# Dividing the attention output by its row sums between two DVE block transposes, with a projection in two halves, in a fused attention and mixture-of-experts kernel

## What is computed

```python
q, k, v = (proj(Wq), proj(Wk), proj(Wv))          # each (b, 16, 512, 8)
q = _l2norm(q); k = _l2norm(k)
sim = einsum('bhid,bhjd->bhij', q, k) * SCALE     # causal mask, SCALE = 8
attn = _softmax(sim)
o = einsum('bhij,bhjd->bhid', attn, v).transpose(0, 2, 1, 3).reshape(b, n, d)
return einsum('bnf,fd->bnd', o, Wo)
```

## Time and profile before

| what | us |
|---|---|
| three runs | 796.7, 798.49, 802.25 (median 798.49) |
| the profiled execution | 802.14 |
| its span, first to last instruction | 800.4 |
| PE busy | 716.7 (90%) |
| DVE busy | 491.1 (61%) |
| ACT busy | 495.4 (62%) |
| POOL busy | 431.9 (54%) |

### The profile page before, as it was taken

How to read it: one execution, slowest core, us unless ns; L and a number is a source line. 1 busy time by engine, 2 the same in 40 slices (tenths; PEclk the granted TensorE clock), 3 DMA queues, 4 the chain that set the end, 5 groups by cost and what they waited for, 6 DMA issues and landing times. The chain is left out here.

```text
span 800.4 us, 19383 instructions
## 1 busy us (share of the span) xinstructions
PE 716.7 (90%) x6151; PEld 447.5 (56%) x6151; DVE 491.1 (61%) x1318; ACT 495.4 (62%) x833; POOL 431.9 (54%) x558
## 2 busy tenths in 40 slices
PE   2777659999999998999979999999989999999986
PEld 2555512333333334999969999999953333333333
DVE  7799795566556754444424444667645766677743
ACT  2566537788887875444424444444457888887873
POOL 4444417666666667576620016476525666666672
PEclk9888859999999998999989999999989999999998
DMA  7665548443354236644422224344414544444331
GB/s 207 211 211 177 171 113 192 82 85 76 92 97 102 66 83 142 204 143 126 141 66 66 72 79 112 99 117 112 111 39 80 70 96 101 100 113 116 65 93 34
DMA packets 170117, 89.20 MB, mean 111 GB/s; under 512 B 77104, under 2 KB 159824, under 8 KB 170064
## 3 DMA queue, kind: packets, MB, share of 16 engines
q1 hardware_dynamic: 161872, 71.74, 36.4%
q0 software_dynamic: 8192, 16.79, 7.3%
HBM read 39.47 MB, written 32.24 MB: 90 GB/s over the span
## 5 line engine op out<-in xcount | busy, mean ns | idle before, releaser
L674 ACT ACTIVATE prob<-psum 128x1024 f32<-128x1024 f32 x320 | 311.0, 1034 | 89.1 <-PE psum L770 83.8
L686 ACT ACTIVATE prob<-psum,prob 128x256 f32<-128x256 f32 x284 | 117.6, 471 | 157.6 <-PE psum L934 156.7
L795 PE MATMUL psum<-prob,v 128*18 128x384 f32 (+2 forms) x2560 | 180.5, 390 | 2.0 <-POOL prob L564 1.0
L557 POOL TENSOR_SCALAR_AFFINE_SELECT prob<-prob 128x512 f32<-128x512 f32 x128 | 88.1, 688 | 134.2 <-ACT prob L674 133.9
L546 POOL DMA_INDIRECT slot_x<-rows,idx x128 | 126.1, 985 | 48.8 <-issue 29.5
L544 POOL DMA_INDIRECT rows<-slot_y,idx x128 | 123.2, 963 | 53.5 <-issue 25.7
L770 PE MATMUL psum<-qks 32*128 32x512 f16 (+3 forms) x1024 | 126.3, 307 | 23.8 <-ACT prob L674 17.7
L946 PEld LDWEIGHTS psum<-prob 128*128 128x128 f32 x1136 | 138.4, 192 | 3.7
L934 PE MATMUL psum<-xs,prob 128*128 128x256 f32 x568 | 138.8, 388 | 0.0
L946 PE MATMUL psum<-prob 128*128 128x128 f32 x1136 | 138.5, 275 | 0.0
L770 PEld LDWEIGHTS psum<-qks 32*128 32x128 f16 x1024 | 33.9, 92 | 162.7 <-ACT prob L674 105.5
(11 more groups left out here) (146 smaller groups left out, 744.5 us busy)
## 6 DMA issues: line engine op xcount, KB each, us to landing
xs<-slot_x SPq DMA_DIRECT2D x71, 128.0 KB
slot_y<-xs SPq DMA_DIRECT2D x71, 128.0 KB
xs<-in_L_attn_x SPq DMA_DIRECT2D x16, 256.0 KB, 3.3
prob<-in_L_ffn_W SPq DMA_DIRECT2D x16, 256.0 KB, 3.1
xn_rows<-xns SPq DMA_DIRECT2D x16, 256.0 KB, 3.5
xn_cols<-xts SPq DMA_DIRECT2D x16, 256.0 KB, 3.5
xt<-xn_cols SPq DMA_DIRECT2D x16, 256.0 KB, 3.5
rows<-xn_rows SPq DMA_DIRECT2D x16, 256.0 KB, 3.2
```

Source lines behind the costliest of these rows:

```text
L557: pool.affine_select(out=p, in_=p, compare_op=ALU.is_ge, fill=0.0, base=0, pattern=[[0, 2], [0, 2], [1, P]], channel_multiplier=-1).then_i ...
L674: act.activation(prob[:, q % 2, KEPT[u], :], score[(q + u) % 2], ACT.Exp, scale=SCALE / UP ** 2).then_inc(exp_done, 1)
L686: act.activation(hs[:, s, c, :], psum[:, 2 * s + c // 2, (c % 2) * FT:(c % 2 + 1) * FT], ACT.Gelu, bias=ws[:, s, B1C + c:B1C + c + 1]).the ...
L795: mm = pe.matmul(ps_o[32 * g:32 * g + VW, first:first + cols], lhs, prob[:, w % 2, KEPT[u], c:c + cols], start=(i == 0 and not odd), stop= ...
```

## The change

- The output of an octet (eight heads) goes to a bank of its own: bank 4 for the first half and bank 7 for the second, so `weigh` waits for the half before the last.
- `copy_o`, `turn_o`, `turn_on` and the DVE copy to `ot` are removed. `divide` now has four DVE instructions for each half: a transpose in 32x32 blocks from PSUM to `by_token`, the reciprocal, the multiplication (now with both inputs in SBUF) into `divided`, and a transpose in 32x32 blocks to `ot[half]`. The two halves keep the layout of the bank, with unused rows between heads.
- `wo` becomes two matrices of 128 rows with zeros in the unused rows; it is filled by 16 small DMAs, which SP issues behind the last stores of stage 1, instead of one DMA near the start. POOL has two more memsets at the start.
- `out_project` has eight matmuls in place of four, and stands at the end of window 2 in place of window 3.
- `divide` of the second half of batch 7 moves into `between`; `add_attention` in window 3 moves ahead of `divide`.
- The computation of `pick` moves from the end of the routing to window 3 of batch 0; its turn on PE goes to window 2 of batch 1, in spare columns of bank 6.

```diff
-            def copy_o(k):
-                act.wait_ge(pv_done, 2 * k + 2)
-                if some(k):
-                    act.wait_ge(otr_done, k)
-                act.copy(osb, ps_o).then_inc(o_evac, 1)
...
             def out_project(b, projected):
-                pe.wait_ge(ot_ready, b + 1)
+                pe.wait_ge(ot_ready, 2 * b + 2)
                 pe.wait_ge(proj_evac, projected)
                 for t in range(TB):
-                    mm = pe.matmul(ps_pa[:, t * D:(t + 1) * D], ot[:, t * P:(t + 1) * P], wo[:],
-                                   start=True, stop=True)
+                    for half in range(2):
+                        mm = pe.matmul(ps_pa[:, t * D:(t + 1) * D], ot[half][:, t * P:(t + 1) * P], wo[:, half, :],
+                                       start=(half == 0), stop=(half == 1))
                 mm.then_inc(outp_done, 1)
...
                     scores(b, par, w, 0)
-                    if w == 1 and not known(b, 0):
-                        if some(2 * b - 1):
-                            pe.wait_ge(norm_done, 2 * b - 1)
-                        turn_o(2 * b - 1)
-                    elif w == 3:
...
-                        turn_o(2 * b)
-                    if known(b, 0) and w == 1:
+                    if known(b, 1) and w == 2:
                         pe.wait_ge(pick_ready, 1)
...
-                    if w == 3 and not known(b, 0):
-                        out_project(b - 1, TB * (b + 1) if last else TB * (b + 2))
                     scores(b, par, w, 3)
                     if weighs:
                         weigh(*before_this, [3, 4])
-                    if w == 1 and not known(b, 0):
-                        turn_on(b - 1)
+                    if w == 2 and not known(b, 0):
+                        if known(b, 1):
+                            pe.wait_ge(wo_in, 16 * H)
+                        out_project(b - 1, TB * (b + 1) if last else TB * (b + 2))
                     scores(b, par, w, 4)
...
-            def divide(k, half):
+            def divide(k, half, projected):
 
-                dve.wait_ge(otr_done, k + 1)
-                o = ps_pc.rearrange("p (t c x) -> p t c x", t=TB, c=QH)
+                dve.wait_ge(pv_done, 2 * k + 2)
                 if some(k):
                     dve.wait_ge(norm_done, k)
-                dve.reciprocal(rs[:], o[:, :, :, DH:VW:DH + 1]).then_inc(rs_done, 1)
+                dve.transpose(by_token, ps_octet[half]).then_inc(o_evac, 1)
+                dve.wait_ge(o_evac, k + 1)
+                dve.reciprocal(rs[:], by_block[:, :, DH:VW:DH + 1]).then_inc(rs_done, 1)
                 dve.wait_ge(rs_done, k + 1)
...
+                dve.tensor_tensor(heads_of(to_block), heads_of(by_block),
+                                  rs[:].rearrange("p j (x a) -> p j x a", a=1).broadcast_to([P, N // 32, 2, DH]),
                                   ALU.mult).then_inc(norm_done, 1)
+                dve.wait_ge(norm_done, k + 1)
+                if some(projected):
+                    dve.wait_ge(outp_done, projected)
+                dve.transpose(ot[half], divided).then_inc(ot_ready, 1)
...
                     elif w == 1:
-                        if not known(b, 0):
-                            divide(2 * b - 1, 1)
+                        if not (known(b, 0) or known(b, HALF)):
+                            divide(2 * b - 1, 1, b - 1)
                         if not last:
                             prepare(b + 1, 1 - par, 1)
-                        if not known(b, 0):
-                            dve.wait_ge(ontr_done, b)
-                            if some(b - 1):
-                                dve.wait_ge(outp_done, b - 1)
-                            dve.tensor_copy(ot, ps_pc).then_inc(ot_ready, 1)
...
             def between():
 
                 mask2(NQ * HALF - 1, NQ - 1)
+                divide(2 * HALF - 1, 1, HALF - 1)
```

More of the change, by code:

```diff
@@ L156, in build @@
         v = sb("v", [P, 2, TB * H, VW])
[L157 to L161, removed]
+        rs = sb("rs", [P, N // 32, 2])
+        turn = sb("turn", [P, 4 * N])
+        by_token = turn[:, 0:N]
+        divided = turn[:, 2 * N:3 * N]
+        ot = [turn[:, N:2 * N], turn[:, 3 * N:4 * N]]
         later = turn[:, 0:T * E * T * E // P // 2].bitcast(F16).rearrange("p (c t e) -> p c t e", t=T, e=E)
@@ L338, in _ @@
             sp.dma_start(wexp[:, :, B2C:WX], b2_all).then_inc(b2_in, 16)
-            sp.wait_ge(zero_made, 1)
+            sp.wait_ge(zero_made, 3)
+            for k in range(H):
+                half, g, j = k // (2 * QH), k // 2 % QH, k % 2
+                r = 32 * g + (DH + 1) * j
+                sp.dma_start(wo[r:r + DH, half, :], Wo[DH * k:DH * (k + 1), :]).then_inc(wo_in, 16)
             spare = slot_x.rearrange("(u p) d -> p u d", p=P)[:, TOPK * T:SLOTS // P, :]
@@ L695, in _ @@
             attention(act, body, between)
-            copy_o(2 * NB - 1)
         @block.tensor
@@ L779, in weigh @@
                     if i == 0:
-                        if not odd and some(2 * b + w // 2):
-                            pe.wait_ge(o_evac, 2 * b + w // 2)
+                        if not odd and some(2 * b + w // 2 - 1):
+                            pe.wait_ge(o_evac, 2 * b + w // 2 - 1)
                         pe.wait_ge(exp_done, UN * n + 3)
@@ L794, in weigh @@
                         lhs = pairs[par][:, kt * H // 2 + pair, odd * (DH + 1):odd * (DH + 1) + VW]
-                        mm = pe.matmul(ps_o[32 * g:32 * g + VW, first:first + cols], lhs,
+                        mm = pe.matmul(ps_octet[w // 2][32 * g:32 * g + VW, first:first + cols], lhs,
                                        prob[:, w % 2, KEPT[u], c:c + cols], start=(i == 0 and not odd),
@@ L963, in _ @@
             weigh(NB - 1, 1, NQ - 1, range(5))
-            pe.wait_ge(norm_done, 2 * NB - 1)
-            turn_o(2 * NB - 1)
-            turn_on(NB - 1)
             pe.wait_ge(added, NB - 1)
@@ L1274, in body @@
                     else:
-                        if some(b):
-                            dve.wait_ge(ontr_done, b)
-                        divide(2 * b, 0)
                         if not known(b, 0):
                             add_attention(b - 1, MOVES * b if second else 0)
+                        divide(2 * b, 0, b)
                     if second and not known(b, HALF) and w in (1, 2):
@@ L1283, in body @@
                         combine(b, par, range(MOVES))
-                    if known(b, 0) and w == 1:
+                    if known(b, 0) and w == 3:
+                        pick_tiles()
+                    if known(b, 1) and w == 1:
                         write_plan()
```

64 lines of the change are left out of this document (25 added, 39 removed).

## The result

| | kernel before | changed kernel |
|---|---|---|
| median of four runs each, us | 798.52 | 810.65 |
| lowest and highest, us | 796.7, 802.25 | 808.14, 811.41 |
| the profiled execution, us | 802.14 | 808.14 |
| its span, us | 800.4 | 806.4 |

The ratio is 1.0141, with a 95% interval from 1.0110 to 1.0171: the change made the kernel slower by 1.4%, where the prediction was 798.8 us and no change. The spans differ by 6.0 us and the medians by 12.1: the profiled execution of before (802.14) lies 3.6 us above its median, near its slowest run, and that of the changed kernel is the fastest of its four, 2.5 us under its median. Of the other 6.1 they say nothing.

What follows compares the result with a forecast made beforehand. PE, coupled to ACT with two units of slack, was taken to set the pace. The terms summed to +0.3 us (-1.3 - 0.4 - 7 x 0.3 + 1.5 - 0.4 + 6 x 0.8 - 1.5 - 0.3): 798.8 us, range 790 to 809.

Steps and rivals of the forecast that it cites:

- The place and the mechanism: End of window 2: PE stands at `out_project` until DVE, with a longer `divide`, copies out tile 3's v.
- the stall of the first half: PE's wait at `out_project` in first-half batches: 0.1 us, for a net of -0.3 us a batch.
- The stall of the second half: PE's wait at `out_project` in batches 9 to 14: 1.2 us mean, for a net of +0.8 us a batch.
- rival C: PE is less busy and its granted clock falls once in a batch: +14 x 1.6 us, 821 us; chance 0.07.
- The gain per batch: PE work falls by 0.7 us a batch; its waits for ACT leave some 0.4 us of that.
- The four added matmuls: Four more float32 matmuls in `out_project` cost PE +1.09 us a batch.
- `pick` in window 2 of batch 1: The later turn of `pick` on PE meets tile 1 already copied and costs nothing.
- Between: Batch 7's last `divide` precedes DVE's first copy of expert weights; the first tile's delay goes through: +1.5 us.
- Batch 15 and the end: Batch 15 loses ACT copies and PE transposes, -1.5 us; the end, `divide` then `out_project`, -0.3 us.
- Transposes on DVE: Each transpose in `divide` takes 0.68 us, within bounds of 0.43 and 1.3 us.
- Rivals A and B: A: PE gain without the stall, 790.9 us, chance 0.22. B: DVE transpose 1.2 us or more, 813 to 827, chance 0.14.
- the start: Batch 0: weighing starts before `pick`, next `prepare` and mask earlier, -1.3 us; one `turn_o` less, -0.4 us.

Runs made afterwards that it cites:

- e1: Changed kernel with `out_project` at the end of window 2 waiting for three of the next batch's tiles, not four: 795.38 us, ratio 0.9968 to the kernel before.
- e3: Changed kernel with the reciprocals in the octet's PSUM bank, so the product has one SBUF input: 803.02 us, ratio 1.0053 to the kernel before.
- e2: Changed kernel with `out_project` back in window 3, ahead of unit 3's scores, still waiting for four tiles: 798.04 us, ratio 0.9991 to the kernel before.
- e4: e1 with `out_project` multiplying only the first half of the heads, four matmuls in place of eight: 783.06 us, ratio 0.9789.
- e9: Kernel before with only `out_project` moved from window 3 to the end of window 2: 794.85 us, ratio 0.9964 to the kernel before.
- e7: Changed kernel with e1's edit, `pick` turned in window 3 of batch 1, and batch 15's combines behind the last `divide`: 792.36 us, ratio 0.9924.

## Why the prediction was wrong

- *The place and the mechanism were right, the sizes weren't.* PE waits at `out_project` for tile 3's v, ended by DVE's L1071, and e1, which takes away only that, gives 15.3 us back. The prediction named this place as the one that decides.
- *The first term that failed: the stall of the first half*, 0.1 against 0.53 to 0.86. It was taken from one idle gap of DVE of 0.99 us, with the product stretched by 0.1 on average. But the average (0.65 us) is over two kinds: mostly 0.51 in window 3, and 0.82 to 0.86 in window 1, the only one that counts. e3, which undoes this stretch of 0.4 us, brings batches 2 to 6 to no stall and 23.86 us, with the help of instructions behind it that were stretched less. The prediction had the row for it, a subtraction with two SBUF inputs at twice its time, and averaged it away. The Trainium skill ("SBUF — State Buffer", the section on two separate sides) calls the port pair that DVE and POOL share an exclusive lock, which the loser waits out in full. The rows agree only roughly: the indirect DMA ends at 650.23 (649.28 + 0.95) and the product 0.30 us later, at 650.53, sooner than the 0.43 that it takes alone. Spans on POOL are rough, and no run tells a lock from sharing. Six batches: 3.8 us of stalls against 0.6.
- *The stall of the second half* was 1.06 to 1.08 in five batches, against 1.2: near, but in part by luck. The product took 0.43 us more than alone where 0.1 was added, and in exchange the subtraction of tile 1, stretched to 0.85 in before, took 0.42 in the changed kernel (at 652.56). Batch 12 had 2.56 and a low clock behind it, 4.6 us over before in place of 0.8. It is more than all of the 3.2 us missed there; the other batches came to 0.6 instead of 0.8. A fall of the clock once in a batch was rival C; in the attention batches after the start it came once.
- *The gain per batch* was 0.4 predicted and 0.49 measured (24.35 to 23.86, e1 and e2). The four added matmuls cost 0.89 (e4) in place of 1.09. That ACT eats part of the gain on PE was foreseen: the waits in the rows went from 1.0 to 1.8 us a batch, predicted 1.3 to 1.65. What the prediction lacked is why. By the rows under e9, some 0.3 of the 0.49 come from the removed `copy_o` on ACT, which stood between two exponentials; moving `out_project` hides that copy as well, so in e9 the place has this gain already and turning on DVE adds only 0.19.
- *`pick` in window 2 of batch 1 was costed at nothing.* The new wait needs tiles 0 and 1 copied out, and PE stood 1.11 us for L1071 there; with the stall of 0.86 the batch took 26.11 us. In e7 it takes 23.99. The prediction took tile 1 as already copied at this place, without a row for it.
- *Between:* the first expert tile starts 1.5 us later, measured from the last mask to DVE's first copy of weights (308.89 to 313.20 before, 306.94 to 312.80 after). But the step that failed is that this goes through: POOL's wait for the rows ends 30.0 us after the mask before and 30.6 after the change, and the projection of batch 9's first tile starts 285.8 and 285.5 us after it. The delay was lost in the waits of that stage.
- *Batch 15 and the end:* -1.8 predicted for both, about +0.9 measured. From the start of batch 14 to PE's last weighing behind the mask (790.46 before, 795.77 after) the changed kernel is 0.9 longer: 0.6 are batch 14's, 0.5 the longer wait for the mask (0.99 in place of 0.47), which leaves -0.2 for the removed copies and transposes of batch 15, where -1.5 was forecast; no run takes that apart. From there to the end it is 0.7 longer, since the last projection came at the low clock (3.65 us, 2.05 before for half as many matmuls, at the low clock too), the upper end of what the prediction had allowed.
- *Transposes on DVE:* 0.71 us each, 0.68 assumed. Rivals A and B on their length fall.
- *The range* ended at 809, by six times the upper stall and 2.5 us, rounded up by one. The first half, `pick` and the end had to share these 2.5 us, and missed by 3.2, 1.1 and 2.6. The misses in the attention batches and at the end (+4.4, +3.2 and +2.6 us in the table) have one sign, since most of them are waits costed at nothing or as an average; those at the start and between (-2.3 and -2.0) have the other and hid part of them in the trace.

What stays open: the medians differ by 12.1 us and the traced spans by 6.0. Executions that were not traced can't be split by batch; low clocks like those at 137.6 (before, about 1.5 us) and in batch 12 (after, 2.5 us) come in one trace and not in another. Why batch 12 is stretched on one chip and not on the other wasn't settled.

## What to carry to other kernels

A wait that moves earlier is priced by the latest producer in that one place: take the duration that its instructions have there, not their mean over all places, and check what data it really needs (here one bank of two, worth 15 us). Work taken off the busiest engine is worth only what the engine coupled to it lets through (0.49 of 0.85 us with `out_project` in window 3, 0.19 of 0.79 in window 2), and the parts of a change don't add up, since two of them can hide the same wait. So measure the change with its waits removed before you call it good. When a step is moved, price each wait that it carries along, also those that come once.

## What the runs showed of the hardware

- A DVE transpose in 32x32 blocks of 128x512 float32 takes 0.71 us, from PSUM or from SBUF alike; the plain copy from PSUM took 0.68.
- A float32 product of 128x256 with two SBUF inputs takes 0.43 us at best and up to 0.86 beside an indirect DMA on POOL; with one of its inputs in PSUM, 0.42 in all 32 cases.
- PE's wait for ACT behind a block of other work doesn't depend on the block's length: 1.11 us after 1.1 us and after 2.0 us. What is fixed at these places is the distance from a unit's scores to the scores two units on, 1.51 us, the start and the length of one exponential on ACT.
- The granted clock dips for some microseconds in some batches, and a stall ahead doesn't decide it: 0.88 over batch 12 behind a stall of 2.56 us, no dip behind the same stall in e3, 0.94 over batch 11 on the other chip behind 1.07. The 16 records of the last projection took 2.02 us (granted clock 1.00) or 3.65 (0.53).
